# Padding rows that carry an index of their own, and scatters of finished tiles without an index bound, in a fused attention and mixture-of-experts block

## The reference

```python
x = x + layernorm(attention_block(layernorm(x), ...))
h = layernorm(x).reshape(-1, 128)                    # 4096 tokens
probs = softmax(h @ router_w.T)
top_w, top_idx = top_k(probs, 2)
w_te = einsum('tk,tke->te', top_w, one_hot(top_idx, 8))
g = einsum('th,eih->tei', h, gate_w)                 # 352 hidden values per expert
u = einsum('th,eih->tei', h, up_w)
y = einsum('tei,ehi,te->th', silu(g) * u, down_w, w_te)
x = x + layernorm(y)
```

## Time and profile before

| | |
|---|---|
| Three runs | 622.0, 619.76 and 620.87 us, median 620.87 us |
| Profiled execution | span 616.4 us from its first to its last instruction; of its device time nothing else is given, and 4.5 us lie between the span and the median |
| Busy | TensorE 86%, ScalarE 64%, VectorE 62%, POOL 57% of the span |
| Expert tiles | from 376 us to 586 us, the last 45 puts from 491 us on |
| Last part (load `ytok`, normalise, store) | from 586 us to 616 us |

### The profile page before, as it was taken

The page is one execution under the profiler, slowest core; times in us unless marked ns, Lnnn a source line. Parts: engine busy times, 40 slices in busy tenths (PEclk is TensorE's granted clock), DMA queues, the critical chain, the costliest instruction groups (busy, mean ns, idle before and its releaser), DMA issues.

```text
span 616.4 us, 13926 instructions
## 1 busy us (share of the span) xinstructions
PE 528.4 (86%) x4585; PEld 387.8 (63%) x4585; DVE 384.0 (62%) x1089; ACT 395.4 (64%) x874; POOL 350.1 (57%) x448
## 2 busy tenths in 40 slices
PE   7868899899998899997898999989999599999170
PEld 5643455456565555654565667879899499999030
DVE  6745583965966839988658866446755335552047
ACT  3468988988878788777888783634544235554025
POOL 4023636555458875278965463764667766665535
PEclk9986999999999999999999999999999879999666
DMA  8756333203223232134546212110222122211074
GB/s 199 119 129 140 103 103 105 78 28 103 78 89 101 90 108 80 42 120 111 150 139 162 70 28 70 45 48 20 67 74 71 46 68 71 59 50 35 16 272 137
DMA packets 48118, 55.88 MB, mean 91 GB/s; under 512 B 7820, under 2 KB 42383, under 8 KB 45888
## 3 DMA queue, kind: packets, MB, share of 16 engines
q1 hardware_dynamic: 43728, 46.52, 27.7%
q0 software_dynamic: 4320, 8.47, 4.1%
HBM read 37.12 MB, written 18.29 MB: 90 GB/s over the span
## 4 chain that ended last, share of the span: by engine, by line
PE 42%; POOL 16%; DVE 15%; issue 11%; ACT 8%; DMA 5%; SPq 2%; DVEq 1%; POOLq 0%; ACTq 0%
PE OA L702 9%; POOL ytok L1696 8%; PE M L743 4%; PE SC L828 4%; PE M L779 3%; ACT arena L947 3%; PE SC L684 3%; POOL slots L1685 3%; POOL IDLE L1690 3%; PE OA L838 2%; PE SC L688 2%; PE M L618 2%; DVE SS L1258 2%; PE M L637 1%; PE SC L694 1%
## 5 line engine op out<-in xcount | busy, mean ns | idle before, releaser
L947 ACT ACTIVATE arena<-SC 128x1024 f32<-128x1024 f32 x160 | 161.7, 1039 | 13.3 <-PE SC L689 11.0
L828 PE MATMUL SC<-arena 128*128 128x128 f32 (+1 forms) x852 | 109.2, 279 | 0.9 <-DVE arena L1439 0.9
L828 PEld LDWEIGHTS SC<-arena 128*128 128x128 f32 (+1 forms) x852 | 101.6, 187 | 1.4 <-DVE arena L1439 1.1
L702 PE MATMUL OA<-arena 128*32 128x256 f32 (+1 forms) x1536 | 90.9, 356 | 6.7 <-DVE arena L422 2.8
L1685 POOL DMA_INDIRECT slots<-XBA,IDX x64 | 72.7, 1136 | 37.0 <-DVE IDX L1383 19.6
L1431 DVE TENSOR_TENSOR arena<-arena,SC 128x256 f32<-128x256 f32 (+1 forms) x142 | 43.5, 348 | 59.7 <-PE SC L828 49.0
L702 PEld LDWEIGHTS OA<-arena 128*32 128x32 f32 x1536 | 39.6, 110 | 46.2 <-issue 24.7
L838 PE MATMUL OA<-arena 128*128 (+1 forms) x426 | 61.1, 280 | 6.2 <-DVE arena L1431 4.2
L1696 POOL DMA_INDIRECT ytok<-YSA,XGA x39 | 40.5, 1039 | 42.9 <-POOL IDLE L1690 22.5
L421 POOL TENSOR_TENSOR arena<-arena 128x512 f32<-128x512 f32 x32 | 42.9, 1340 | 33.9 <-ACT arena L947 33.3
L838 PEld LDWEIGHTS OA<-arena 128*128 128x128 f32 (+1 forms) x426 | 54.4, 195 | 7.9 <-issue 7.9
(11 more groups left out here) (238 smaller groups left out, 1073.8 us busy)
## 6 DMA issues: line engine op xcount, KB each, us to landing
arena<-parts SPq DMA_DIRECT2D x90, 192.0 KB
parts<-arena SPq DMA_DIRECT2D x16, 384.0 KB
arena<-ytok SPq DMA_DIRECT2D x8, 512.0 KB, 6.7
XGA<-slots SPq DMA_DIRECT2D x39, 65.0 KB
arena<-slots SPq DMA_DIRECT2D x32, 65.0 KB
X<-in_L_attn_x SPq DMA_DIRECT2D x4, 512.0 KB, 5.2
arena<-toe SPq DMA_DIRECT2D x16, 128.0 KB, 6.0
out<-X SPq DMA_DIRECT2D x8, 256.0 KB, 2.4
```

The lines of the kernel that those rows point to most:

```text
L702: mm = pe.matmul(OA[32 * j:32 * j + 32, q0:q0 + n], vals[:, t, 32 * h:32 * h + 32], probs(j), start=first, stop=last, skip_group_check=True)
L828: mm = pe.matmul(SC[0:n, r % 2, 512 * m + P * c:512 * m + P * (c + 1)], WSEL[s % 4][:, I * m + i0:I * m + i0 + n], XGT[r % 2], start=True, ...
L947: act.activation(EB[u], SC[:, n % 2, :], ACT.Exp).then_inc(exp_done, 1)
```

## The change

- `NO_ROW` and `PADX` go. Two views (`PADV`) of the SBUF buffers `XGA` and `WSX`, each 128 partitions x 8 rows of 130 values, are filled by POOL at the start with two memsets and two iotas: zeros, and in the index place a number of its own for every row, from `2 * NTOK` up.
- SP copies both to DRAM behind `stack(0)`: one to a new table `pads`, one to eight dummy tiles behind the regions of `slots`. Before the last sequence's `stack`, it waits for them.
- The eight pads behind the experts' rows are copied from `pads` (DRAM) to `slots` (DRAM), where before they came from SBUF.
- `ytok` is longer by 2048 rows, into which padding rows are written. Each tile beyond those in use reads a dummy tile of its own (`LAST_ROW`).
- The indirect DMA of `put` names no bound.
- `const_rdy` is raised by a memset of `IDLE` that waits for `nib_rdy`.

```diff
-NO_ROW = 1 << 20
...
-    slots_d = nc.dram_tensor("slots", [(E * REGION + P), ROW], F32)
-    ytok_d = nc.dram_tensor("ytok", [2 * NTOK, D], F32)
+    UNUSED = STILES - 2 * NTOK // P
+    LAST_ROW = DUMMY + (UNUSED - 1) * P
+    assert UNUSED <= E
+    slots_d = nc.dram_tensor("slots", [E * REGION + E * P, ROW], F32)
+    pads_d = nc.dram_tensor("pads", [E * P, ROW], F32)
+    ytok_d = nc.dram_tensor("ytok", [2 * NTOK + 2 * E * P, D], F32)
...
-        PADX = sb("PADX", [P, ROW])
...
+        PADV = [a[:, 0:E * ROW].rearrange("p (e c) -> p e c", c=ROW) for a in (XGA, WSX)]
...
                 if b == NB - 1:
+                    sp.wait_ge(dummy_out, 32)
                     for i in range(NHI):
                         stage(i)
...
             stack(0)
-            sp.wait_ge(const_rdy, 1)
-            sp.dma_start(slots_d.ap()[DUMMY:DUMMY + P, :], PADX[:, :]).then_inc(dummy_out, 16)
+            sp.wait_ge(dummy_rdy, 2)
+            for table, v in zip((pads_d.ap(), slots_d.ap()[DUMMY:DUMMY + E * P, :]), PADV):
+                sp.dma_start(table.rearrange("(e p) c -> p e c", p=P), v).then_inc(dummy_out, 16)
...
-                row = sp.value_load(SRI[0:1, 0, s:s + 1], min_val=0, max_val=DUMMY)
+                row = sp.value_load(SRI[0:1, 0, s:s + 1], min_val=0, max_val=LAST_ROW)
...
-                    sp.dma_start(slots_d.ap()[bass.ds(row, P), :], PADX[:, :]).then_inc(pad_out, 16)
+                    e = s - PADS_AT
+                    sp.dma_start(slots_d.ap()[bass.ds(row, P), :], pads_d.ap()[P * e:P * (e + 1), :]).then_inc(pad_out, 16)
...
             sp.wait_ge(pad_out, 16 * E)
-            sp.wait_ge(dummy_out, 16)
...
-            yt_v = ytok_d.ap().rearrange("(b p k t) d -> b p (k t d)", p=P, k=2, t=T)
+            yt_v = ytok_d.ap()[0:2 * NTOK, :].rearrange("(b p k t) d -> b p (k t d)", p=P, k=2, t=T)
...
-                dve.tensor_scalar(SRI[:, 0, s0:s0 + n], row, float(DUMMY), None, ALU.min)
+                dve.tensor_scalar(SRI[:, 0, s0:s0 + n], row, float(LAST_ROW), None, ALU.min)
...
-            pool.memset(PADX[:, :], 0.0)
...
-            pool.iota(PADX[:, D + 1:D + 2].bitcast(I32), pattern=[[0, 1]], base=NO_ROW, channel_multiplier=0).then_inc(const_rdy, 1)
+            pool.wait_ge(nib_rdy, 1)
+            pool.memset(IDLE[:, :], 0.0).then_inc(const_rdy, 1)
...
             pool.wait_ge(v2_const, 2)
+
+            for k, v in enumerate(PADV):
+                link(pool.memset(v, 0.0))
+                pool.iota(v[:, :, D + 1].bitcast(I32), pattern=[[P, E]], base=2 * NTOK + k * E * P, channel_multiplier=1
+                          ).then_inc(dummy_rdy, 1)
...
                                         out_offset=bass.IndirectOffsetOnAxis(ap=XG[r][:, D + 1:D + 2].bitcast(I32), axis=0),
-                                        in_=YS[r], in_offset=None, bounds_check=2 * NTOK - 1, oob_is_err=False
-                                        ).then_inc(ys_out[r], 16)
+                                        in_=YS[r], in_offset=None).then_inc(ys_out[r], 16)
```

More of the change, by code:

```diff
@@ L288, in block_kernel @@
         scattered = [sem("scattered0"), sem("scattered1")]
-        dummy_out = sem("dummy_out")
+        dummy_rdy, dummy_out = sem("dummy_rdy"), sem("dummy_out")
         pad_rdy = sem("pad_rdy")
```

## The result

The changed kernel took 603.51 us (median of four executions, 600.28 to 605.99) beside 620.51 for the kernel before: a ratio of 0.972, 95% interval 0.9681 to 0.9759. That is 17 us less, where the forecast had 28 (592.9 us), and 1 us above the top of the range (602.5). The profiled execution took 605.99 us; its span is 604.3 us.

The account below looks back on a forecast made before the run. POOL's puts were taken to set the pace from about 490 us on. Terms -17.2 -9.5 +0.2 -1.9 +0.4 = -28.0 us took 620.87 to 592.9 us, range 589.5 to 602.5.

Parts of the forecast that it names:

- Point 1: Puts behind tile 40: without a bound each step falls from 2.11 to 1.62 us, POOL catches up, -17.2 us.
- Point 2: Gate at tile 40, which waits for all scatters: eleven cheaper puts bring the last scatter 5.4 us earlier.
- Point 3: Root that POOL computes near 409 us: 2.45 us earlier, plus 1.6 us of half clock avoided, together 4.1 us.
- Points 4 and 5: Last put lands later with all its rows, +0.2 us; the last part's first matmuls get full clock, -1.9 us.
- Point 6: Kernel start: POOL's two new wide memsets may hold VectorE's small operations; +0.4 us, between 0 and 1.8.
- Point 7: Early SP and DMA queues: two 532 KB transfers replace one of 65 KB, covered by slack, 0 us.
- the experts' own pace: Tiles 40 to 70 are evicted every 2.1 us, the pace left once POOL's puts step faster.
- Rival C: Puts cannot follow each other faster than they land, about 2.08 us, so the pace stays: 621 us, chance 0.03.
- Rival D: Unbounded puts take POOL longer because every row is written: some 50 us slower, 670 or more, chance 0.03.
- A: The 0.49 us ahead of each put is not the bound's and stays: 621.5 us, chance 0.04.
- B: DRAM-to-DRAM pads land late and hold the gate at tile 40, losing 9.5 us: 602.4 us, chance 0.09.

Follow-up runs that it names:

- e1_again: The changed kernel run again without an edit, on chip 0: 594.24 us, ratio 0.9566.
- e12: The changed kernel with a bound at the last spare row on every put and no `MEMSET` ahead of it, chip 10: 616.43 us.
- e4: The changed kernel with a second `MEMSET` of `IDLE` ahead of each put, no bound, chip 0: 618.88 us, ratio 0.9987.
- e11_before: The kernel before the change, run again for its trace, chip 10: 620.45 us, ratio 1.0002.
- e2: The changed kernel with a bound back on all puts, at the last spare row so nothing is dropped, chip 0: 620.20 us, ratio 1.0002.
- e3: The changed kernel with the old bound back on all puts, so padding rows are dropped again, chip 0: 619.08 us, ratio 0.9991.
- e7: The changed kernel without the `MEMSET` ahead of every put and of the last 32 scatters, chip 11: 624.97 us, ratio 1.0088.
- e10: The changed kernel with the `MEMSET` ahead of each put 384 columns wide instead of 128, chip 10: 602.66 us, ratio 0.9703.
- e13: The changed kernel with a 384-column `MEMSET` ahead of puts 0 to 49 and the old 128-column one from put 50, chip 1: 602.90 us.
- e16: The changed kernel with the `MEMSET` ahead of each put 256 columns wide instead of 128, chip 1: 598.35 us, ratio 0.9667.
- e5: The changed kernel with a bound at the last spare row back on puts 0 to 25 alone, chip 11: 609.45 us, ratio 0.9828.
- e9: The changed kernel run again without an edit, on chip 10: 607.52 us, ratio 0.9777.
- e15: The changed kernel with the old bound on every put, dropping padding rows, and no `MEMSET` ahead of puts, chip 1: 621.73 us.

## Why the prediction was right, and where it was wrong

The sum in the first profile: span 604.3 against 616.4, 12.1 us less. POOL's lag behind the last eviction gave 16.7 us (17.5 to 0.75), the last part 1.5 (from the last put's start to the end 32.6 to 31.1 us), and the eviction of tile 70 came 6.1 us later instead of 9.5 earlier. -16.7 -1.5 +6.1 = -12.1. (The medians differ by 17.0: the profiled execution of the changed kernel was the longest of its four.)

*Point 1, the step: right.* 17.2 us were forecast and 16.7 came, by the mechanism named; in e1_again POOL draws level at put 58 (forecast: 59), at 1.62 us a put on average (51.7 us over 32), the forecast's own number. Only the reason given for the 0.49 us, a register just written, does not hold: e12 has the same MOVE and pays 0.03 us, e4 has none and pays 0.49. The cost comes with the wait for the `MEMSET` just ahead.

*Point 2, the gate: right in e1_again, nearly in size.* From the first to the last of the last 16 scatters POOL takes 41.2 us (442.18 to 483.41) where it took 46.2 (442.65 to 488.84): 5.0 us less, where the forecast had 5.4 for the 11 puts. The last scatter itself came 5.4 us earlier where points 2 and 3 together had 9.5, since the stage began 2.4 us later and point 3 gave less. TensorE's wait at tile 40 fell from 10.4 us (e11_before) to 4.4 us (e1_again), from their timelines of TensorE:

```profile
496.58 0.48 PE L819 MATMUL M<-IDN,arena 128*128 128x128 f32 x1 [10.38 <-DMA arena<-slots]
```

```profile
488.95 0.47 PE L825 MATMUL M<-IDN,arena 128*128 128x128 f32 x1 [4.36 <-DMA arena<-slots]
```

That may also be why the kernel before hardly shows the pauses it has. In its first profile 2.3 us before L838 stand beside a wait of 8.06 us at the gate, in e11_before 0.5 beside 10.4: nearly the same sum, as if the wait at the gate absorbed them. With two profiles this is no more than a fit. What the runs show is that the change shortened the cover (10.4 to 4.4 us) and enlarged what it had to cover.

*Point 3, the root: right in mechanism, too large, and lost in the sum.* VectorE's wait for the root fell from 6.34 to 4.65 us in the first profile, 1.7 us where 2.45 were forecast, and the half clock behind it is gone:

```profile
412.10 1.12 DVE L1326 SCALAR_TENSOR_TENSOR A<-M,RZ,Y 128x128 f32<-128x128 f32 x4 [4.65 <-POOL RZ L1680]
```

In all the root gave 2.8 us of the forecast 4.1: tile 9 is evicted at 419.19 for 418.53, from a start 3.5 us later (e1_again: 418.07, from 2.4 us later). The later start is the other loss: the first put starts at 390.18 for 386.71, so the stage itself began 3.5 us later. At 340 to 347 us the granted clock was at its lower level, which it was not before (in e1_again for 3.4 us, in e11_before not at all). I had given the whole stretch before the experts +0.4 us. Over 20 profiles of kernels with and without the edit the first put starts anywhere from 385.9 to 391.5 us (387.8 in e2, 388.0 in e11), so this is within the spread of single executions and cannot be laid to the edit (the kernel before has only two of the profiles, 386.7 and 388.0). A sum made against one profile carries it: this term should have had bounds of some 3 us on either side.

*Points 4, 5 and 6: right.* Points 4 and 5 had -1.7 us, and from the last put to the end it is 1.5 us less (1.7 in e1_again), by the mechanisms named: the last put lands in 2.25 us for 2.08, and the first matmuls of L940 take half the time:

```profile
579.65 2.00 PE SC L940 x4
```

Point 6 had +0.4, and the start shows nothing measurable (e2, e3). (It has POOL idle until 60; in the trace of the kernel before POOL works again at 31.13. Nothing hangs on it.) Point 7 had 0, and e3 agrees.

*The step that failed: "the experts' own pace".* Point 1 set it at 2.1 us a tile from a trace in which puts never stood closer than 1.96 us, and the whole sum took it as a property of TensorE that a faster POOL cannot touch: points 2 and 3 had tile 40 evicted "by 494.1 (503.64 less 9.5)", and no rival put a price on what denser DMAs do to the other engines. Puts 1.47 us apart made TensorE pause, on chips 1, 10 and 11 and in the first measurement. In the profile after, tile 40's eviction ended at 508.47, not at 494.1. From tile to tile (end of the eviction; the forecast for tile 15 is 432.60 less the 4.1 of point 3):

| tile | before | forecast | after | behind the forecast | e1_again | behind the forecast |
|---|---|---|---|---|---|---|
| 15 | 432.60 | 428.5 | 433.26 | 4.8 | 432.14 | 3.6 |
| 40 | 503.64 | 494.1 | 508.47 | 14.3 | 498.64 | 4.5 |
| 70 | 566.33 | 556.8 | 572.48 | 15.7 | 561.33 | 4.5 |

Of the 15.7 us, 4.8 were lost ahead of tile 15 (the later start and the root), 9.6 between tiles 15 and 40, where TensorE paused (11.1 us of waits before L844 for 2.3, and half the clock behind the first, less the 2.7 us that the forecast had left at the gate), and 1.3 behind tile 40, at one more pause. So most of the loss lies ahead of the gate, where POOL's new pace met TensorE at work, and hardly any in tiles 40 to 70, for which the pace had been read.

Where the pauses did not come (e1_again) the miss is 4.5 us, all but 0.9 of it ahead of tile 15, and the time 594.2 for 592.9 us. That the time is nearer than the tiles is in part luck. Beside the kernel before in its own job (619.69) the gain is 25.4 us of the forecast 28.0. And the execution from which the sum was drawn (span 616.4) was shorter than the usual one: in the later runs the time stands 1.7 or 1.8 us above the span, which would put it at some 618.2 us (an estimate), under the median of 620.9.

Rival C was wrong in its own form (puts do follow closer than they land, 1.26 us apart in e7 against 2.25 to landing). It drew on the page "DMA: Bandwidth & Descriptors" of the Trainium skill ("Anatomy of one DMA"), which gives a DMA from GpSimd a fixed cost of about 2.0 us; the trace agrees for one DMA, and shows that several are under way at once. But C had the right object, the pace of indirect DMAs; the limit lies in what it does to others, not to POOL. Rival D's point, a longer `DMA_INDIRECT`, did not come: its median is 967 ns. A and B did not come either. B's 602.4 us lie near the 603.5 measured, but by chance: late pads would show as a wait for the load of tile 40, and in the profile after TensorE has none of 0.8 us or more there.

Shown by the runs: that POOL's step between indirect DMAs decides the gain (e1, e2 and e4, in one job); that on chips 10, 11 and 1 a wider step brings fewer pauses, whether a `MEMSET` (e10, e13, e16) or the bound (e5 near 435 us, e11_before against e9) makes it wider; that padding rows (e15) are not the cause of the pauses. Not shown: what inside the chip holds the semaphore updates back; whether it is the distance between two DMAs or how long and how even a row of them is; why chip 0 had none of it at 1.47 us in four executions (a second job there was not run), for which reason the runs on chip 0 (e2 to e4) prove nothing about pauses; and whether 1.57 us holds on chips other than chip 1.

## What to carry to other kernels

A pause ahead of an indirect DMA that looks like waste may be what keeps the other engines running. Before you shorten the step of a queue that is the bound, look up how closely its DMAs have ever stood in the trace, and treat anything closer as unmeasured, with a price on the engines that do not use that queue. Read that price tile by tile from the engine that should become the bound: here tiles 15 to 40 held it. When an engine has been the bound for long, speed it up only as far as the next one needs: 1.57 us against TensorE's 2.11 gave as much as the fastest job with 1.47 within 1%, and did so on a chip where 1.47 cost 13 us. A gain that depends on the chip shows only in several jobs; one profile, and the first result, would have told half of it.

## What was not expected of the hardware

- Indirect DMAs from POOL 1.26 to 1.47 us apart hold up semaphore updates of TensorE and of the DMA engines, on three chips of four, in bursts 0.7 to 1.4 us apart (after: 505.8 to 508.0 us; e7: 462.7 to 465.5), for 1 to 6.6 us at a time (e7's chain has one of 6.55 from 493.21 on). In the profile it reads as "another core or an unknown queue" or "remote" on ScalarE's evictions, and as idle time of TensorE that ends with an engine long done.
- It differs by chip or job: 0.6 us of such waits (L844, 430 to 515 us) on chip 0, 13 to 18 us on chips 1, 10 and 11, for one and the same kernel.
- The bound of an indirect DMA costs 0.49 us behind a `MEMSET` that POOL waited for (e2 against e1), and 0.03 us without one (e12 against e7). A second `MEMSET` of 0.2 us costs the same 0.49 us (e4).
